# One eight-chunk loop for layer norm, transposes and all four projections, with affine, gates and norms in slots 2 to 5

## The chip, the core and the metric

The kernel runs on one core of a Trainium2 chip. A core has five engines with queues of their own: PE (TensorE, matrix products into PSUM), DVE (VectorE), ACT (ScalarE), POOL (GpSimd) and SP (SyncE, which here only issues DMAs). Each engine runs its instructions strictly in program order; between engines the order is made by semaphores. The metric is the device time of one execution in microseconds (us).

## The reference, cut to what matters

The input is 16 sequences of 256 tokens with 128 features, 4096 tokens in all. The output is the input plus an attention block plus a product-key expert block, both on the layer norm of the input.

```python
xn  = (x - mean) / sqrt(var + 1e-5)
# attention: 16 heads of 8 features
q   = xn @ Wq + bq
lat = xn @ Wl + bl;  k = lat @ Wk + bk;  v = lat @ Wv + bv
attn = softmax(q k^T / sqrt(8));  a = (attn v) @ Wo + bo
# experts: 8 heads, queries of 32 features
f   = xn @ fWq + fbq                       # 256 columns
f   = (f - mean(f)) / sqrt(var(f) + 1e-5) * gamma + beta   # over all tokens and heads
f0, f1 = l2norm of either half of f        # 16 features each
s0, s1 = f0 @ l2norm(key0)^T, f1 @ l2norm(key1)^T; top 4 of 32 in each
w   = softmax over the 16 sums;  idx = pairs of the top 4
out = sum_k w_k * gelu(down[idx_k] . xn) * up[idx_k]
return x + a + out
```

The mean and variance of `f` run over all tokens: no query can be scaled before the last chunk is projected.

## The kernel before: how it is tiled and what sets its order

The 4096 tokens are cut into eight chunks of 512 (`NC = 8`, `CH = 512`, four tiles of 128 tokens each). After a prologue loop over the chunks comes a software pipeline of "slots": slot n handles pair n of heads of the 128 pairs (`NPAIR * B`), eight to a sequence. Every engine's program holds both, written out by hand; nothing is reordered.

**Prologue loop.** For each chunk c DVE makes the mean and variance (lines 746 to 753), ACT the root (337), DVE the reciprocal and the shift `nm` (731, 733); ACT and DVE normalise two tiles each into `xn_sb` (326 and 739); PE transposes (462) into `psX`, ACT copies the result to `xnT` (334). One chunk later PE multiplies with fWq into `psF` (469), two halves r = 0, 1, which ACT copies to `fqT` (331) and of which DVE takes statistics with `bn_stats` (761). The matrices Wl and Wk, Wv are folded into `wkv` at c = 2 to 4 (473 to 478, copied by ACT at 317 to 319). Only chunks 0 and 1 are projected to q and k in or right behind this loop.

**Projections.** `project_qk(c)` and `project_v(c)` are three products with `wq_sb` and `wkv` (438, 441, 451) in PSUM `psQ`, `psK`, `psV`. DVE moves q and k to `q32` (`q_ev` 703, `k_ev` 710). Each fp32 value is then cut into three bf16 parts: ACT writes the first (303, in `first_parts`), POOL the residue `r32` (940, in `residues`), ACT the second (310, `second_parts`), POOL the third of q (942), DVE the third of k (`lo_k`, 714). `r32` has one buffer for q and one for k, so POOL's residue of a chunk waits until the third parts of the chunk before are made. SP writes the parts of a chunk to DRAM (`spill`, 245, six DMAs) and loads them back as rows of the heads (`load`, 262, twelve DMAs for a sequence). The parts have two buffers: `first_parts(c)` waits for `spill(c - 2)`. SP's queue, which the change leaves as it is, starts so:

```python
            spill(0)
            load(0)
            load(1)
            for c in range(1, NC):
                spill(c)
```

**Slots.** In each, PE makes the scores S of a pair (`si`, 526), DVE takes the row maxima `negm` (837), later (from slot 11) PE makes the transposed scores (586), ACT the exponential (413), PE the product with v (607). Chunks 2 to 7 are projected in slots 1 to 6, with their parts on ACT, POOL and DVE. Slot 0 solves for the scale of `f` (`bn_solve`, 802 to 813). In slots 0 to 7 DVE scales chunk `slot` of `fqT` in place (828, the affine), ACT squares it (367), PE sums the squares (`norms`, 539), and PE and ACT make the gates gelu(down . xn) (564, 362); `inverse_squares` (777, 780) turns sums of squares to inverses, a pair of chunks at a time. Until slot 10 the scores have one buffer `SI[0]`, because `SI[1]` holds v and the gates. POOL's residues stand in slots 0 to 6, and at slot 8 POOL adds the output bias to all of x in one instruction (954). From slot 8 on the experts' selection runs on DVE (881, 901), POOL (976 to 1019, 1039) and PE (634, 651), and `mpart` (1028, 1030) hands the maxima of a sequence over to PE (622).

Of the kernel before, what the change touches and what calls it, by code (L numbers as in the profile page):

```python
# [46 lines left out]
def program(nc, x, Wq, bq, Wl, bl, Wk, bk, Wv, bv, Wo, bo,  # L47
# [35 lines left out]
    with ctx:  # L83
# [45 lines left out]
        sq = Eb[:, 1, :].rearrange("p (r n) -> p r n", r=2)  # L129
# [160 lines left out]
        def _(act):  # L290
# [7 lines left out]
            def first_parts(c):  # L298
                if c >= 2:
                    act.wait_ge(s[f"spill{c % 2}"], 16 * NSPILL * (c // 2))  # L300
                for t, nm in enumerate(("q", "k")):
                    act.wait_ge(s[nm + "_ev"], c + 1)
                    A(parts[:, c % 2, t, 0, :], q32[:, t, :], ACT.Copy).then_inc(s["hi_" + nm], 1)  # L303
                    if t == 0 and c >= 1:
                        v_rows(c)

            def second_parts(c):
                for t, nm in enumerate(("q", "k")):
                    act.wait_ge(s["r_" + nm], c + 1)
                    A(parts[:, c % 2, t, 1, :], r32[:, t, :], ACT.Copy).then_inc(s["mid_" + nm], 1)  # L310

            for c in range(-1, NC + 2):
                if c == 4:

                    act.wait_ge(s["wkv"], 1)
                    act.wait_ge(s["w"], NW)
                    A(wkv[:, :, :], psW[:, 0:2 * D].rearrange("p (a d) -> p a d", a=2), ACT.Copy)
                    A(vecs[:, 8:9], psW[:, 2 * D:2 * D + 1], ACT.Identity, bias=vecs[:, 1:2])
                    A(vecs[:, 9:10], psW[:, 2 * D + 1:2 * D + 2], ACT.Identity, bias=vecs[:, 7:8]).then_inc(s["wkv_ev"], 1)
                if 0 <= c < NC:  # L320
# [7 lines left out]
                if c >= 2:  # L328
                    for r in range(2):
                        act.wait_ge(s["f"], 2 * (c - 2) + r + 1)  # L330
                        A(fqT[:, r, (c - 2) * CH:(c - 1) * CH], psF[c % 2][r], ACT.Copy).then_inc(s["f_ev"], 1)
# [746 lines left out]
```

## Time and profile before

| | us |
|---|---|
| median of three timed runs | 402.14 (401.37 to 403.36) |
| the profiled execution | 396.66 |
| its span, first to last instruction | 395.0 |

| engine | busy us | share of the span |
|---|---|---|
| PE | 330.2 | 84% |
| DVE | 347.4 | 88% |
| POOL | 248.0 | 63% |
| ACT | 244.3 | 62% |

The page has one line for each engine, with the span in 40 equal slices of 9.9 us; a digit is the busy share in tenths, and PEclk is TensorE's granted clock in tenths of full speed:

```profile
DVE  7769569999996999999999999999999999999571
ACT  2666438766746566666666666665756665656671
POOL 6003034776795676777586686767577677768780
PEclk9996989999858999999999999999999999999999
```

The first nine or ten slices are the prologue and slots 0 to 7, on which the change works; after some fourteen the pattern repeats.

### The profile page before, as it was taken

How to read it: one execution, taken by the hardware profiler on the slowest of the kernel's cores; microseconds unless marked ns; L12 is line 12 of the kernel's file. 1: busy time of each engine (PE TensorE's matmuls, PEld its weight loads, DVE VectorE, ACT ScalarE, POOL GpSimd, SP SyncE). 2: the span in 40 equal slices, each digit the busy share in tenths (PEclk: the TensorE clock that was granted, in tenths of full speed). 3: DMA queues.
4: the chain of work that ended last, by engine and by line, in shares of the span. 5: the costliest groups of instructions: out<-in, count | busy, mean ns of one | idle time of the engine just before them, and what ended most of it. 6: DMA issues, size and time to landing. Idle time of an engine off the chain costs nothing.

```text
span 395.0 us, 9652 instructions
## 1 busy us (share of the span) xinstructions
PE 330.2 (84%) x3080; PEld 175.2 (44%) x3080; DVE 347.4 (88%) x1446; ACT 244.3 (62%) x371; POOL 248.0 (63%) x527
## 2 busy tenths in 40 slices
PE   1877778885679898988989898898989898898874
PEld 0443444441325454544545454455445454454443
DVE  7769569999996999999999999999999999999571
ACT  2666438766746566666666666665756665656671
POOL 6003034776795676777586686767577677768780
PEclk9996989999858999999999999999999999999999
DMA  6401693445664150414235160515323060000000
GB/s 189 111 0 27 124 114 109 116 135 152 110 80 71 14 81 5 95 32 67 64 35 81 18 95 14 85 44 57 68 28 97 3 95 17 2 17 2 28 17 13
DMA packets 45886, 24.81 MB, mean 63 GB/s; under 512 B 5452, under 2 KB 45708, under 8 KB 45836
## 3 DMA queue, kind: packets, MB, share of 16 engines
q1 hardware_dynamic: 45836, 24.20, 33.1%
q8 instruction: 24, 0.39, 0.5%
q14 instruction: 26, 0.21, 0.2%
HBM read 15.54 MB, written 8.39 MB: 61 GB/s over the span
## 4 chain that ended last, share of the span: by engine, by line
PE 44%; DVE 20%; issue 5%; POOL 5%; ACT 2%; POOLq 0%; DVEq 0%
PE bank L607 11%; DVE negm L837 10%; PE bank L651 8%; PE bank L634 8%; PE SI L526 6%; DVE r_sb L901 6%; PE SJ L586 5%; PE bank L676 2%; ACT s_sb L381 2%; PE bank L677 2%; PE bank L678 2%; DVE rden L854 1%; DVE fqT L828 1%; POOL prod L1039 1%; PE bank L622 1%
## 5 line engine op out<-in xcount | busy, mean ns | idle before, releaser
L837 DVE TENSOR_REDUCE negm<-SI 128x4 f32<-128x1024 f32 x128 | 154.2, 1214 | 2.5 <-PE SI L526 2.5
L413 ACT ACTIVATE Eb<-SJ 128x1024 f32<-128x1024 f32 x128 | 130.3, 1018 | 32.0 <-PE SJ L586 31.8
L1039 POOL TENSOR_TENSOR prod<-r_sb,a 128x1024 f32<-128x1024 f32 x31 | 60.3, 1945 | 25.9 <-issue 25.9
L607 PE MATMUL bank<-Eb,vhat 128*18 128x256 f32 x1024 | 69.6, 390 | 0.0
L526 PE MATMUL SI<-KS,QS 48*128 48x256 bf16 x512 | 51.2, 279 | 19.5 <-DVE negm L837 17.3
L586 PE MATMUL SJ<-QS,KS 50*128 50x256 bf16 x512 | 51.7, 281 | 8.3 <-ACT Eb L413 8.1
L940 POOL TENSOR_TENSOR Eb<-Eb,parts 128x512 f32<-128x512 f32 x16 | 20.3, 1285 | 54.2 <-ACT parts L303 54.2
L881 DVE MAX8 top<-s_sb 128x8 f32<-128x32 f32 x512 | 50.4, 174 | 4.4 <-ACT s_sb L381 4.4
L901 DVE MATCH_REPLACE8 r_sb<-top,s_sb 128x36 f32<-128x36 f32 x256 | 43.1, 180 | 0.0
L526 PEld LDWEIGHTS SI<-KS,QS 48*128 48x128 bf16 x512 | 18.1, 96 | 54.5 <-issue 45.0
L651 PE MATMUL bank<-cst,prod 128*128 128x128 f32 x256 | 34.5, 278 | 4.2 <-ACT s_sb L381 3.7
L634 PE MATMUL bank<-kblk,fqT 128*128 128x256 f32 x128 | 37.1, 413 | 0.3
L607 PEld LDWEIGHTS bank<-Eb,vhat 128*18 128x18 f32 x1024 | 24.0, 98 | 27.3 <-issue 15.2
L651 PEld LDWEIGHTS bank<-cst,prod 128*128 128x128 f32 x256 | 27.5, 141 | 12.2 <-POOL prod L1039 7.0
L381 ACT ACTIVATE s_sb<-bank 128x512 f32<-128x512 f32 x32 | 19.1, 597 | 22.1 <-PE bank L634 20.1
L586 PEld LDWEIGHTS SJ<-QS,KS 50*128 50x128 bf16 x512 | 14.7, 95 | 36.4 <-ACT Eb L413 22.3
L634 PEld LDWEIGHTS bank<-kblk,fqT 128*128 128x128 f32 x128 | 22.2, 193 | 9.4 <-issue 3.8
L962 POOL COPY top<-top 128x32 f32<-128x32 f32 x32 | 6.7, 209 | 29.3 <-DVE top L881 29.3
L403 ACT ACTIVATE ysb<-bank 128x256 f32<-128x256 f32 x16 | 6.1, 383 | 28.4 <-PE bank L678 28.4
L846 DVE TENSOR_TENSOR wgT<-bank,xnT 128x256 f32<-128x256 f32 x16 | 6.8, 424 | 15.3 <-PE bank L651 15.3
L901 DVE MATCH_VALUE_LOAD r_sb<-top,s_sb 128x8 f32 x256 | 20.1, 79 | 0.0
L979 POOL TENSOR_TENSOR z_sb<-s_sb,rn 128x512 f32<-128x512 f32 x16 | 16.9, 1058 | 0.0
(149 smaller groups left out, 586.0 us busy)
## 6 DMA issues: line engine op xcount, KB each, us to landing
qk_parts<-parts SPq DMA_DIRECT2D x48, 128.0 KB, 2.4
QS<-qk_parts SPq DMA_DIRECT2D x32, 96.0 KB
KS<-qk_parts SPq DMA_DIRECT2D x32, 96.0 KB
x_sb<-L_attn_x SPq DMA_DIRECT2D x8, 256.0 KB, 3.7
QS<-qk_parts SPq DMA_DIRECT2D x32, 64.0 KB
KS<-qk_parts SPq DMA_DIRECT2D x32, 64.0 KB
out<-ysb SPq DMA_DIRECT2D x16, 128.0 KB, 4.2
QS<-qk_parts SPq DMA_DIRECT2D x32, 32.0 KB
```

The costliest lines, as they stand in the source:

```text
L381: A(s_sb[:, FH * t:FH * (t + 1), :, 0:NK].rearrange("p h a k -> p (h a) k"), psM.rearrange("p (g k) -> p g k", k=NK), ACT.Copy).then_inc(s ...
L413: A(Eb[:, n % 4, :], SJ[:, :], ACT.Exp).then_inc(s["ex"], 1)
L526: last = mm(si_buffer(n)[:, (e * BT + t) * S:(e * BT + t + 1) * S], QS[r, b % RING, pr, t * P:(t + 1) * P], KS[r, b % RING, pr, :], start= ...
L586: last = mm(SJ[:, (e * BT + t) * S:(e * BT + t + 1) * S], KS[r, b % RING, pr, t * P:(t + 1) * P], QS[r, b % RING, pr, :], start=True, stop ...
L607: last = mm(psO[32 * c:32 * c + 2 * VC, (q % 2) * S:(q % 2 + 1) * S], vhat[:, v0:v0 + 2 * VC], Eb[:, (2 * g + c // 2) % 4, e0:e0 + S], sta ...
L634: last = mm(psM[:, 256 * r:256 * (r + 1)], fqT[:, r, tok:tok + P], kblk[:, :, :].rearrange("p g k -> p (g k)"), start=True, stop=True)
L651: last = mm(psM[:, t * P:(t + 1) * P], prod[:, t, h, :, :].rearrange("p i j -> p (i j)"), ident, start=(h == 0), stop=(h == FH - 1), is_tr ...
L837: V.tensor_reduce(negm[:, bb % 2, :, :, pr].rearrange("p t e -> p e t"), si_buffer(slot)[:, :].rearrange("p (e t j) -> p e t j", e=2, j=S) ...
L881: last = V.max(top8[:, h, a, :], s_sb[:, h, a, 0:NK])
L901: last = V.match_replace(r_sb[:, h, :], top4[:, h, :], s_sb[:, h, 1, :], NEG)
L940: TT(r32[:, t, :], q32[:, t, :], parts[:, c % 2, t, 0, :], ALU.subtract).then_inc(s["r_" + nm], 1)
L1039: TT(prod[:, t, :, :, :], r_sb[:, hs, 0:NK].unsqueeze(2).to_broadcast([P, FH, TOP, NK]), a0[:, hs, :].unsqueeze(3).to_broadcast([P, FH, TO ...
```

## The change

One loop over the eight chunks now holds the layer norm, the transposes and all four projections: q, k and v of chunk c - 1 are made in iteration c, fWq of chunk c in iteration c itself. The splits into parts, `lo_k` and POOL's residues are in that loop as well (before, those of chunks 1 to 7 stood behind it or in the slots). `wkv` is folded at c = 0 and 1. The affine, the gates, the squares and the sums of squares of all chunks are done in slots 2 to 5, two chunks a slot. Scores have two buffers from the start and `si(n + 1)` is issued in slot n. `psF` has three buffers, `sq` has two. `bn_solve` is cut in two, in slots 0 and 1. POOL's addition of the bias to x stands at slot 0, right behind the residues of chunk 7. SP's queue isn't changed.

The diff, cut to its core:

```diff
             # ACT
+            deviations(0)
+            for c in range(NC + 1):
+                if c < NC:
                     act.wait_ge(s["nm"], c + 1)
...
                 if c + 1 < NC:
+                    deviations(c + 1)
+                if c < NC:
+                    act.wait_ge(s["xT"], c + 1)
+                    A(xnT[:, c * CH:(c + 1) * CH], psX[c % 2], ACT.Copy).then_inc(s["xnT"], 1)
+                if c == 1:
+                    act.wait_ge(s["wkv"], 1)
...
+                if c >= 1:
+                    first_part(c - 1, 0)
+                    first_part(c - 1, 1)
+                    v_rows(c - 1)
+                if c < NC:
+                    features(c, 0)
+                if c >= 1:
+                    second_part(c - 1, 0)
+                if c < NC:
+                    features(c, 1)
+                if c >= 1:
+                    second_part(c - 1, 1)
...
+            def first_part(c, t):
+                nm = "qk"[t]
+                act.wait_ge(s[nm + "_ev"], c + 1)
+                if c >= 2 and t == 0:
                     act.wait_ge(s[f"spill{c % 2}"], 16 * NSPILL * (c // 2))
...
+                if FILTER <= slot < FILTER + NC // 2:
+                    pair = (2 * (slot - FILTER), 2 * (slot - FILTER) + 1)
+                    for c in pair:
+                        act.wait_ge(s["g"], c + 1)
+                        A(gT[:, c * CH:(c + 1) * CH], psG[c % 2], ACT.Gelu).then_inc(s["g_ev"], 1)
...
+                    for c in pair:
+                        act.wait_ge(s["ff"], c + 1)
+                        if c >= 2:
+                            act.wait_ge(s["n2"], c - 1)
+                        A(sq[c % 2], fqT[:, :, c * CH:(c + 1) * CH], ACT.Square).then_inc(s["sq"], 1)
             # PE, in the loop, behind the transposes of chunk c
+                if c >= 1:
+                    project_qk(c - 1)
+                    project_v(c - 1)
+                if c < NC:
+                    pe.wait_ge(s["xnT"], c + 1)
+                    for r in range(2):
+                        i = 2 * c + r
+                        if i >= 3:
+                            pe.wait_ge(s["f_ev"], i - 2)
+                        mm(psF[i % 3], fwq_sb[:, r * P:(r + 1) * P], xnT[:, c * CH:(c + 1) * CH],
+                           start=True, stop=True).then_inc(s["f"], 1)
             # PE, in the slots
+            si(0)
             for slot in range(NSLOT):
...
+                if FILTER <= slot < FILTER + NC // 2:
+                    for c in (2 * (slot - FILTER), 2 * (slot - FILTER) + 1):
...
+                        mm(psG[c % 2], downT[:, :], xnT[:, c * CH:(c + 1) * CH], start=True, stop=True).then_inc(s["g"], 1)
...
+                if slot < NPAIR * B - 1:
                     si(slot + 1)
+                if FILTER <= slot < FILTER + NC // 2:
+                    norms(2 * (slot - FILTER))
+                    norms(2 * (slot - FILTER) + 1)
             # DVE, in the loop
                 if c + 1 < NC:
+                    moments(c + 1)
+                if c >= 1:
+                    q_ev(c - 1)
+                    k_ev(c - 1)
                     for r in range(2):
+                        dve.wait_ge(s["f_ev"], 2 * (c - 1) + r + 1)
+                        V.bn_stats(fst[:, r, c - 1, :], fqT[:, r, (c - 1) * CH:c * CH]).then_inc(s["f_st"], 1)
...
+                if c >= 2:
+                    lo_k(c - 2)
...
+            lo_k(NC - 1)
             # DVE, in the slots
+                if FILTER <= slot < FILTER + NC // 2:
+                    for c in (2 * (slot - FILTER), 2 * (slot - FILTER) + 1):
+                        fc = fqT[:, :, c * CH:(c + 1) * CH]
...
+                if slot == 0:
+                    bn_shift()
+                if slot == 1:
+                    bn_scale()
+                if FILTER < slot <= FILTER + NC // 2:
+                    inverse_squares(slot - FILTER - 1)
             # POOL
-            residues(0)
+            for c in range(NC):
+                residues(c)
             for slot in range(NSLOT):
                 k = slot % 8
                 b = slot // 8 - 1
-                if slot < NC - 1:
-                    residues(slot + 1)
-                if slot == NC:
+                if slot == 0:
                     pool.wait_ge(s["w2"], NW2)
                     pool.wait_ge(s["xn"], NC)
```

## Rows read from the trace of the kernel before

**Rows 1.** Windows: stretch, length, busy us (xcount) of PE, PEld, DVE, ACT, POOL; clock, DMA.

```profile
0.00:55.00 55.00, 35.13 (x113) 18.50 (x114) 39.04 (x148) 28.91 (x65) 12.85 (x14) 0.93 0.44 91
55.00:97.00 42.00, 33.08 (x242) 16.24 (x244) 41.82 (x53) 29.89 (x46) 24.18 (x20) 0.97 0.50 126
...
137.00:345.00 208.00, 189.27 (x2032) 102.45 (x2028) 199.14 (x918) 134.60 (x191) 149.78 (x363) 1.00 0.31 51
```

**Rows 2.** Timeline (start us, us, engine, instruction): DVE's maxima of slots 8, 24, 32.

```profile
96.79 1.23 DVE L837 TENSOR_REDUCE negm<-SI 128x4 f32<-128x1024 f32 x1
...
136.70 1.21 DVE L837 TENSOR_REDUCE negm<-SI 128x4 f32<-128x1024 f32 x1
...
154.31 1.22 DVE L837 TENSOR_REDUCE negm<-SI 128x4 f32<-128x1024 f32 x1
```

**Rows 3.** Timeline, prologue: first norm, first fWq products, copy of wkv, q product.

```profile
7.19 0.88 ACT L326 ACTIVATE Eb<-x_sb,ve,rs 128x128 f32<-128x128 f32 x2 [0.44 <-DVE ve L733]
...
11.59 3.62 PE L469 MATMUL SI<-xnT,fwq_sb 128*128 128x512 f32 x4
...
22.54 0.38 ACT L317 ACTIVATE wkv<-SJ 128x256 f32<-128x256 f32 x1 [2.81 <-PE SJ L478]
...
27.31 1.02 PE L438 MATMUL SJ<-xnT,wq_sb 128*128 128x512 f32 x2
```

**Rows 4.** Groups of DVE instructions, 0 to 100 us: count | busy us, mean ns | idle.

```profile
L828 DVE TENSOR_SCALAR fqT<-fqT,bnv 128x512 f32<-128x512 f32 x16 | 16.8, 1091 | 0.0
...
L761 DVE BATCH_NORM_STATS2 fst<-fqT 128x6 f32<-128x512 f32 x16 | 10.4, 682 | 2.7 <-ACT fqT L331 2.7
L746 DVE BATCH_NORM_STATS2 st<-x_sb 128x6 f32<-128x128 f32 x32 | 6.9, 276 | 0.0
L703 DVE TENSOR_SCALAR Eb<-SJ,vecs 128x512 f32<-128x512 f32 x8 | 5.9, 739 | 0.5 <-PE SJ L438 0.5
...
L714 DVE TENSOR_TENSOR parts<-Eb,parts 128x512 bf16<-128x512 f32 x8 | 5.7, 717 | 0.0
L739 DVE TENSOR_SCALAR Eb<-x_sb,mv,rs 128x128 f32<-128x128 f32 x16 | 4.8, 340 | 0.0
```

**Rows 5.** Single lines and timeline: DVE beside POOL instructions (durations min/median/max in ns).

```profile
L733 DVE SCALAR_TENSOR_TENSOR ve<-mv,rs x8: 161/161/1016, 7.0 to 35.9; 128x4 f32<-128x4 f32 x8
...
35.71 1.15 POOL L942 TENSOR_TENSOR parts<-Eb,parts 128x512 bf16<-128x512 f32 x1 [3.58 <-ACT parts L310]
35.87 1.02 DVE L733 SCALAR_TENSOR_TENSOR ve<-mv,rs 128x4 f32<-128x4 f32 x1
...
L828 DVE TENSOR_SCALAR fqT<-fqT,bnv x16: 533/1345/1385, 55.5 to 93.7; 128x512 f32<-128x512 f32 x16
...
381.06 2.89 POOL L1039 TENSOR_TENSOR prod<-r_sb,a 128x1024 f32<-128x1024 f32 x1
...
382.22 1.76 DVE L921 TENSOR_TENSOR prod<-prod,p0r 128x8 f32<-128x8 f32 x1
```

**Rows 6.** Timeline: POOL's addition of the bias to x.

```profile
97.16 8.83 POOL L954 TENSOR_TENSOR x_sb<-x_sb,bo_sb 128x4096 f32<-128x4096 f32 x1
```

**Rows 7.** Timeline of SP's queue: spill of chunk 0, first and last of the loads.

```profile
36.89 4.12 SPq L245 DMA_DIRECT2D qk_parts<-parts  x6
42.76 1.03 SPq L262 DMA_DIRECT2D QS<-qk_parts  x3
...
52.04 1.24 SPq L262 DMA_DIRECT2D KS<-qk_parts  x3
```

**Rows 8.** Groups of ACT instructions, 0 to 100 us: count | busy us, mean ns | idle.

```profile
L303 ACT ACTIVATE parts<-Eb 128x512 bf16<-128x512 f32 x16 | 9.9, 620 | 2.1 <-DVE Eb L710 1.6 <-DVE Eb L703 0.5
L367 ACT ACTIVATE Eb<-fqT 128x1024 f32<-128x1024 f32 x8 | 8.4, 1052 | 5.1 <-DVE fqT L828 2.8 <-PE bank L539 2.2
```

**Rows 9.** Timeline, slots: sums of squares, and PE behind POOL's maxima of sequence 1.

```profile
59.01 0.64 PE L539 MATMUL bank<-Eb,cst 128*32 128x128 f32 x16
...
118.16 0.39 PE L622 MATMUL bank<-cst,mpart 128*32 128x128 bf16 x2 [1.19 <-POOL mpart L1030]
```

More of the change, by code:

```diff
@@ L296, in v_rows, with second_part, features, deviations @@
                 A(v_tiles(c, c + 1)[:, :, 0:DH], psV.rearrange("p (n v) -> p n v", v=DH), ACT.Copy).then_inc(s["v_ev"], 1)
-            def first_parts(c):
-                if c >= 2:
+            def first_part(c, t):
+                nm = "qk"[t]
+                act.wait_ge(s[nm + "_ev"], c + 1)
+                if c >= 2 and t == 0:
                     act.wait_ge(s[f"spill{c % 2}"], 16 * NSPILL * (c // 2))
[L301 to L320, printed above, removed]
+                A(parts[:, c % 2, t, 0, :], q32[:, t, :], ACT.Copy).then_inc(s["hi_" + nm], 1)
+            def second_part(c, t):
+                nm = "qk"[t]
+                act.wait_ge(s["r_" + nm], c + 1)
+                A(parts[:, c % 2, t, 1, :], r32[:, t, :], ACT.Copy).then_inc(s["mid_" + nm], 1)
+            def features(c, r):
+                i = 2 * c + r
+                act.wait_ge(s["f"], i + 1)
+                A(fqT[:, r, c * CH:(c + 1) * CH], psF[i % 3], ACT.Copy).then_inc(s["f_ev"], 1)
+            def deviations(c):
+                act.wait_ge(s["var"], c + 1)
+                A(sd[:, TC * c:TC * (c + 1)], ve[:, TC * c:TC * (c + 1)], ACT.Sqrt).then_inc(s["std"], 1)
+            deviations(0)
+            for c in range(NC + 1):
+                if c < NC:
                     act.wait_ge(s["nm"], c + 1)
@@ L419, in _ @@
                     A(mT[:, :], psM[0:2 * H, 0:S], ACT.Copy).then_inc(s["mt_ev"], 1)
[L420 removed]
+                if slot == FILTER + NC // 2:
                     act.wait_ge(s["n2r"], NC // 2)
@@ L580, in _ @@
                         pe.wait_ge(s["kone"], 32)
-                        pe.wait_ge(s["q_ev"], NC)
-                        pe.wait_ge(s["k_ev"], NC)
+                        pe.wait_ge(s["g_ev"], NC)
                     for t in range(BT):
@@ L726, in unit_keys, with moments @@
                 last.then_inc(s["krep"], 1)
-            for c in range(-1, NC + 3):
-                if 0 <= c < NC:
+            def moments(c):
+                dve.wait_ge(s_x[c], 16)
+                tiles = range(TC * c, TC * (c + 1))
+                for n in tiles:
+                    last = V.bn_stats(st6[:, n, :], x_sb[:, n, :])
+                last.then_inc(s["stats"], 1)
+                dve.wait_ge(s["stats"], c + 1)
+                for n in tiles:
+                    last = V.bn_aggr(mv[:, n, :], st6[:, n, :])
+                last.then_inc(s["aggr"], 1)
+                dve.wait_ge(s["aggr"], c + 1)
+                V.tensor_scalar(ve[:, TC * c:TC * (c + 1)], mv[:, TC * c:TC * (c + 1), 1],
+                                LN_EPS, None, ALU.add).then_inc(s["var"], 1)
+            moments(0)
+            for c in range(NC + 1):
+                if c < NC:
                     dve.wait_ge(s["std"], c + 1)
@@ L796, in _, with bn_shift @@
                             grp.unsqueeze(2).to_broadcast([P, 8, NK]), ALU.mult).then_inc(s["kblk"], 1)
-            k_ev(1)
-            def bn_solve():
+            lo_k(NC - 1)
+            def bn_shift():
                 dve.wait_ge(s["ba"], 2)
```

175 lines of the change are left out of this document (46 added, 129 removed).

## The prediction

> **What bounds the kernel now.** I read the page's engine lines first, then the busy times of four long windows, then the timeline of the prologue and the first slots engine by engine, and last the single DVE lines whose longest duration is far above their shortest. In the repeating part, DVE is busy 199.14 of 208 us [rows 1]: it is the bound, and a sequence of eight slots takes 154.31 - 136.70 = 17.6 us [rows 2]. The change doesn't touch that part. DVE works in program order and has nothing to make up with, so whatever shifts slot 8 on DVE shifts the end. I therefore forecast when the maxima of slot 8 start: at 96.79 before [rows 2]. Slots 8 to 24 then take 39.9 us, 4.7 more than two sequences of 17.6.
>
> Between 55 and 97 us DVE seems full as well, 41.82 of 42 us [rows 1], but a part of that is waiting. An affine instruction takes 0.53 us at best and 1.35 at the median [rows 5]; sixteen take 16.8 us [rows 4] where 8.5 would do. The long ones stand beside POOL's residues. The same holds for tiny ones: the shift `nm` takes 0.16 us, and 1.02 once, when it came 0.16 us after a POOL instruction of 1.15 us had begun; it ended with it [rows 5]. Near the end, DVE's sum on 128x8 elements needs 1.76 us while POOL's product, itself held up by DVE, runs until 383.95 [rows 5]. So a DVE instruction of these kinds (scaling SBUF to SBUF, or two inputs in SBUF) and one of POOL exclude each other. The maxima, `bn_stats` and everything that reads PSUM don't wait.
>
> **The change part by part.** All starts below are us from the start of the span; a(c) is when ACT starts to normalise chunk c.
>
> *The first chunks.* ACT starts at 7.19 as before [rows 3]. Its queue now holds both copies of `features(0)` ahead of chunk 1. The four records of the first fWq products took 3.62 us [rows 3], at about half the rate of later ones (1.02 us for two [rows 3]). Transposes end near 9.3, the copy near 9.9, the products at 13.5, the copy, `wlT` and then a(1) at 14.4 (9.7 before). From there: norm 0.9, transposes 0.8, folding of wkv 1.2, its copy at 17.3 (22.54 before [rows 3]) and two small ones until 18.1, then q, k and v on PE (about 2.9) until 21, and five copies of 0.55 to 0.62 us [rows 8]: a(2) = 24.2. Bounds 23 to 26, by PE's rate.
>
> *The loop's period.* DVE does per chunk 4 x 0.28 + 2 x 0.34 for the norm, 2 x 0.74 for `q_ev` and `k_ev`, 2 x 0.68 for statistics, 0.67 to 0.72 for `lo_k` [rows 4] and seven small ops of about 0.16 [rows 5]: 6.4 us, about 6.2 start to start. ACT has nine such ops of 0.5 to 0.6 plus the norm, 6.0 us [rows 8], less than DVE. POOL's two residues and the third part of q are 1.15 us each [rows 5]. They exclude DVE's `nm`, its two normalised tiles and `lo_k`. By program order `lo_k` of chunk c - 2 releases the residue of k of chunk c - 1. DVE's next step is the reciprocal and then `nm`, which finds that residue running (about 1.0 us left, as in [rows 5]); then the third part of q gets in and the normalised tiles wait 1.1 us. I take 1.8 of these 2.1 us: period 8.0. Bounds 6.2 (no wait falls badly) and 8.6. Before, these waits were in the affine, 8.3 us in all.
>
> *SP's queue.* It is unchanged, but its neighbours moved. `spill(0)` can end only when `lo_k(0)` is done, which is last in DVE's iteration 2: a(2) + 6.4 = 30.6. Three DMAs (half of 4.12 us [rows 7]) and landing (42.76 - 41.01 = 1.75 [rows 7]) make 34.4. Then come 24 loads, which took from 42.76 to 53.28 = 10.5 us to issue [rows 7], then `spill(1)`, 4.1 + 1.75: landed at 50.8. ACT's first part of chunk 3 writes into the buffer that `spill(1)` reads. It is due in iteration 4, at a(4) + 3.75 = 24.2 + 16.0 + 3.75 = 44. It waits 6.9 us, and behind it in ACT's queue stand v, `features(4)` and the norm of chunk 5, for which PE and DVE wait. Before, the first parts of chunk 3 stood in slot 2, far behind the loads, which were hidden. So a(5) = 50.8 + 4.25 = 55.1, a(6) = 62.6 (DVE has caught up, one period of 7.5), a(7) = 70.6. A faster loop only waits longer here: only three periods count. Bounds of the wait: 3 (loads issue faster) and 10 us.
>
> *The end of the loop.* `q_ev(7)` ends 9.2 us after a(7). Then a first part (0.65), POOL's residue of q (1.15), `lo_k(6)` (0.7), the residue of k and the third part of q (2 x 1.15 and handovers): POOL is free at a(7) + 14.8 = 85.4. What POOL does next is the addition to x, 8.83 us [rows 6]. Before, it ran from 97.16, where DVE only had maxima, a reciprocal, top-4 searches and reads of PSUM, none of which waited. Now DVE's next ops are `lo_k(7)` and `bn_shift`: two inputs in SBUF, or a scaling in SBUF. They wait until 94.2, about 8 us. PE can run only two scores ahead. The longest such wait that the trace shows is 1.76 us [rows 5]; that it holds for one of 8.83 is the step I have to extrapolate. Bounds 0 and 8.7; I take 8, because each wait shown went on to the end of the POOL instruction.
>
> The Trainium skill, SBUF — State Buffer, section "Who interferes with whom", states that VectorE and GpSimd share one pair of SBUF ports by an exclusive lock that is held for the whole instruction, and that a VectorE instruction with two SBUF inputs or in a two-port mode takes part in it. By that rule the wait is the full rest of the 8.83 us; by a wait capped at the 1.76 us of the trace the sum would be about 6 us lower.
>
> *Slots 0 to 7.* The rest of slot 0 takes 0.65 us, slot 1 starts at 94.9. Slots 2 to 5 hold on DVE 4 x 0.53 [rows 5] + 1.2 + 1.25 = 4.6 us at most; the affine no longer meets residues, which saves its 8.3 us. But PE and ACT pass the ball within each slot: two gate products (2 x 0.95), a gelu (0.6), two squares (2 x 1.0 [rows 8]), sums of squares (0.64 [rows 9]) = 5.15 us, and the next gate products stand behind these sums. So slots 1 to 7 take 1.6 + 4 x 5.15 + 1.25 (inverse) + 1.2 = 24.65, and 0.5 for PE starting at its lower clock (1.2 GHz) after the idle stretch. Bounds 20 (DVE alone) and 30 (PE at that clock throughout). Slot 8 starts at 120.0: 23.2 us later than before.
>
> *Slots 8 to 24.* One inverse (1.25) is no longer here, and POOL is free, so that its chain to `mpart`, behind which PE stood at 118.16 [rows 9], starts some 1.5 us earlier. Of the 4.7 us of excess I give back 2.7; bounds 0 and 4.7.
>
> **Sum.** +23.2 - 2.7 = +20.5 us. On the profiled execution: 396.66 + 20.5 = 417.2 (span 395.0, 1.7 lie around it). The timed runs' median is 402.14, 5.5 above the profiled one; I add the same difference there: **422.6**.
>
> **The rivals.**
> - *The long addition doesn't hold DVE.* Everything else as forecast; DVE resumes when the third part of q is done, 7.9 us earlier: 414.7. For it: no row shows a hold beyond 1.76 us. Against it: all shown waits end with the POOL instruction.
> - *The spill doesn't hold the loop.* If DMAs are issued in a way that `spill(1)` lands before 44 us, 6.9 us fall away: 415.7. Against it: SP is in order and its 10.5 us are in the trace.
> - *The loop keeps DVE fed, and it comes out faster.* DVE was busy 39.04 + 41.82 us up to 97 [rows 1]; without the 8.3 us of the affine's waits and some 2 of others, and with one more inverse, its own work up to slot 8 is about 72 us. Before, slot 8 started at 96.8, so some 25 us were waiting. If the loop's waits overlap (period 6.2, no stall by SP or POOL) some 18 us remain: slot 8 at 90, -6.8 - 2.7 = -9.5 us, 392.6. The point from which it decides: DVE must wait less than 27 us in all before slot 8; my forecast has 48. For it: before, DVE idled 16 of the first 55 us [rows 1] because the loop had too little work for it, and now the loop has more. Against it: the in-order queues above.
> - *PE stays at the lower clock through slots 2 to 5.* Each such slot takes 7.2 instead of 5.15 us: +8, 430.6. For it: PE idles for about 8 us right before.
>
> **How the numbers follow.** Forecast 0.62, the addition not holding 0.17, the spill not holding 0.10, PE's clock 0.05, faster 0.06. Both of the first two rivals at once, with a short period (-5), give 403 or so; that is the low side of the cases. The forecast's own bounds: period -5/+2, slots -4/+4, spill -4/+3, last term -2/+2.7. Range for 8 in 10: 407 to 431. A measurement of this kernel can tell about 0.5% from no change. Slower 0.91, the same 0.03 (the mildest corner of the bounds), faster 0.06.
>
> **What would show it.** In the timeline after: ACT's first part of chunk 3 idle for some 7 us with a DMA as releaser near 44 to 51 us; DVE's `lo_k(7)` or the first scaling of `bn_shift` with a duration of 7 to 9 us, ending with POOL's 8.83 us; affines of 0.53 us in slots 2 to 5; `nm` with durations around 1 us; maxima of slot 8 near 120. Wrong would be: a wait of under 2 us beside the long addition, a period near 6, or slot 8 before 105.

## The result and the profile after

The kernel after takes 428.35 us (median of four runs, 426.86 to 432.6) where the kernel before takes 401.75 on the same chip (396.86 to 403.36): ratio 1.072 [1.059, 1.086], +26.6 us. Forecast were 422.6 us and +20.5. The profiled execution took 428.03 us (span 426.4) against 396.66 (395.0) before, so between the two traces lie 31.4 us. Executions of one kernel spread over 4 to 9 us, the slower ones at a lower granted clock (before: 396.6 us at 0.965, 403.7 at 0.945), so a few us between two traces or medians can come from that alone; the ratios leave out runs more than 1.5% above the quickest of their kernel.

The engine lines of the page after (40 slices of 10.7 us, busy share in tenths):

```profile
DVE  7077817679868899999999999999999999999571
ACT  2366156541562666665666656766667656666671
POOL 5043134376000766877677676776767767777790
PEclk9998868885696699999999999999999999999999
```

DVE's unbroken run of nines starts at slice 15, 149 us (before: slice 14 of 9.9 us, 128 us). Ahead of it stand gaps: DVE shows a 1 in slice 6 (53 to 64 us), PEclk falls to 6 in slice 6 to 5 and 6 in slices 10 and 11 (96 to 117 us) and to 6 in slices 13 and 14, and POOL has nothing to do in slices 11 to 13. The windows after, with the columns of [rows 1]: the loop from a(2) on, the stretch of the long addition, slots 1 to 8, and the part that repeats.

```profile
26.40:93.30 66.90, 42.74 (x148) 23.79 (x148) 43.16 (x111) 35.45 (x72) 24.30 (x22) 0.85 0.48 104
93.30:102.60 9.30, 0.22 (x4) 0.00 (x0) 9.27 (x4) 0.00 (x0) 9.28 (x2) 0.52 0.38 103
102.60:132.00 29.40, 21.04 (x184) 9.54 (x184) 21.48 (x40) 15.75 (x20) 0.46 (x2) 0.79 0.00 1
...
172.00:380.00 208.00, 189.06 (x2030) 102.95 (x2030) 199.09 (x934) 133.19 (x188) 150.47 (x371) 1.00 0.31 51
```

DVE is busy 199.09 of 208 us in the repeating part, 199.14 before [rows 1]: nothing was lost or won there. In the loop DVE is busy 43.16 of 66.9 us, PE 42.74 and ACT 35.45: none of them is full. In the second row DVE shows 9.27 us busy with four instructions, and PE all but stands still (0.22 us) at a granted clock of 0.52.

The timeline after, single rows of ACT, SP, POOL, DVE and PE (start us, duration us, engine, line, instruction, [idle before, releaser]):

```profile
26.42 0.88 ACT L324 ACTIVATE Eb<-x_sb,ve,rs 128x128 f32<-128x128 f32 x2
...
26.80 1.92 SPq L242 DMA_DIRECT2D qk_parts<-parts  x3
...
32.33 1.80 SPq L242 DMA_DIRECT2D qk_parts<-parts  x3
35.88 1.03 SPq L259 DMA_DIRECT2D QS<-qk_parts  x3
...
44.27 1.50 SPq L259 DMA_DIRECT2D KS<-qk_parts  x3
...
54.87 1.15 ACT L300 ACTIVATE parts<-Eb 128x512 bf16<-128x512 f32 x2 [8.52 <-DMA qk_parts<-parts]
...
88.56 1.15 ACT L300 ACTIVATE parts<-Eb 128x512 bf16<-128x512 f32 x2 [1.69 <-DMA qk_parts<-parts]
...
93.33 9.25 POOL L947 TENSOR_TENSOR x_sb<-x_sb,bo_sb 128x4096 f32<-128x4096 f32 x1
...
95.15 7.45 DVE L799 TENSOR_SCALAR bnv<-bnv 128x2 f32<-128x2 f32 x1
102.64 0.16 DVE L800 TENSOR_TENSOR bnv<-bnv 128x2 f32<-128x2 f32 x1
...
104.86 3.78 PE L559 MATMUL SJ<-xnT,downT 128*128 128x512 f32 x4
...
112.23 2.93 PE L559 MATMUL SJ<-xnT,downT 128*128 128x512 f32 x4
...
118.31 1.98 PE L559 MATMUL SJ<-xnT,downT 128*128 128x512 f32 x4
...
131.97 1.23 DVE L831 TENSOR_REDUCE negm<-SI 128x4 f32<-128x1024 f32 x1 [0.89 <-PE SI L527]
...
167.93 1.22 DVE L831 TENSOR_REDUCE negm<-SI 128x4 f32<-128x1024 f32 x1
```

The last two rows answer to [rows 2]: the maxima of slots 8 and 24 start at 131.97 and 167.93, 35.2 and 31.2 us later than before. So the whole loss arises before slot 8, and 4.0 us of it come back by slot 24. The SP rows answer to [rows 7] (the two groups of three are the first spill, q and k), the POOL row to [rows 6], the row at 26.42 to the a(2) of the prediction.

Two DVE lines after that answer to [rows 5] and [rows 4] (durations min/median/max in ns, first and last start):

```profile
L824 DVE TENSOR_SCALAR fqT<-fqT,bnv x16: 448/542/548, 105.4 to 120.9; 128x512 f32<-128x512 f32 x16
L749 DVE TENSOR_SCALAR Eb<-x_sb,mv,rs x16: 335/765/1193, 7.1 to 77.4; 128x128 f32<-128x128 f32 x16
```

The affine (L824) takes 0.54 us where its median was 1.35, because no residue runs beside it any more. The normalised tiles (L749) now meet the residues instead: their total goes from 4.8 us [rows 4] to 11.6 for sixteen.

### The profile page after: what moved, and what is told of

It is laid out like the page before. It is cut to its first block, busy times and chain, and to the rows that moved or that the text cites. A ratio compares the mean times of both kernels' runs of the same rounds, so it can differ in the third digit from the quotient of the medians.

```text
span 426.4 us, 9652 instructions
## 1 busy us (share of the span) xinstructions
PE 337.2 (79%) x3080; PEld 180.6 (42%) x3080; DVE 353.2 (83%) x1446; ACT 245.0 (57%) x371; POOL 245.1 (57%) x527
## 4 chain that ended last, share of the span: by engine, by line
PE 53%; DVE 21%; ACT 9%; issue 8%; POOL 4%; SPq 3%; DMA 2%; POOLq 0%; ACTq 0%; DVEq 0%
PE bank L601 10%; DVE negm L831 9%; PE bank L629 8%; PE bank L646 7%; PE SI L527 6%; DVE r_sb L895 5%; PE SJ L580 5%; PE SJ L559 2%; ACT s_sb L386 2%; PE bank L671 2%; SPq L259 2%; PE SJ L444 2%; DMA qk_parts<-parts 2%; PE SJ L447 2%; DVE bnv L799 2%
## 5 line engine op out<-in xcount | busy, mean ns | idle before, releaser
L419 ACT ACTIVATE Eb<-SJ 128x1024 f32<-128x1024 f32 x128 | 130.5, 1019 | 32.8 <-PE SJ L580 32.7
L601 PE MATMUL bank<-Eb,vhat 128*18 128x256 f32 x1024 | 68.6, 386 | 0.0
L934 POOL TENSOR_TENSOR Eb<-Eb,parts 128x512 f32<-128x512 f32 x16 | 18.5, 1160 | 58.9 <-ACT parts L300 50.0
L527 PEld LDWEIGHTS SI<-KS,QS 48*128 48x128 bf16 x512 | 18.3, 96 | 51.5 <-issue 44.0
L386 ACT ACTIVATE s_sb<-bank 128x512 f32<-128x512 f32 x32 | 19.1, 598 | 24.6 <-PE bank L629 22.7
L698 DVE TENSOR_SCALAR Eb<-SJ,vecs 128x512 f32<-128x512 f32 x8 | 6.0, 750 | 28.0 <-PE SJ L444 28.0
L955 POOL COPY top<-top 128x32 f32<-128x32 f32 x32 | 6.8, 211 | 35.5 <-DVE top L875 35.5
L629 PEld LDWEIGHTS bank<-kblk,fqT 128*128 128x128 f32 x128 | 22.7, 197 | 9.7 <-issue 3.8
L300 ACT ACTIVATE parts<-Eb 128x512 bf16<-128x512 f32 x16 | 9.9, 629 | 24.7 <-DMA qk_parts<-parts 10.2
L408 ACT ACTIVATE ysb<-bank 128x256 f32<-128x256 f32 x16 | 6.2, 385 | 28.4 <-PE bank L673 28.4
L1021 POOL CAST mpart<-negm 128x32 bf16<-128x32 f32 x16 | 3.4, 212 | 31.3 <-DVE negm L831 31.3
```

The costliest lines, as they stand in the source:

```text
L386: A(s_sb[:, FH * t:FH * (t + 1), :, 0:NK].rearrange("p h a k -> p (h a) k"), psM.rearrange("p (g k) -> p g k", k=NK), ACT.Copy).then_inc(s ...
L419: A(Eb[:, n % 4, :], SJ[:, :], ACT.Exp).then_inc(s["ex"], 1)
L527: last = mm(SI[n % 2][:, (e * BT + t) * S:(e * BT + t + 1) * S], QS[r, b % RING, pr, t * P:(t + 1) * P], KS[r, b % RING, pr, :], start=Tru ...
L601: last = mm(psO[32 * c:32 * c + 2 * VC, (q % 2) * S:(q % 2 + 1) * S], vhat[:, v0:v0 + 2 * VC], Eb[:, (2 * g + c // 2) % 4, e0:e0 + S], sta ...
L629: last = mm(psM[:, 256 * r:256 * (r + 1)], fqT[:, r, tok:tok + P], kblk[:, :, :].rearrange("p g k -> p (g k)"), start=True, stop=True)
L934: TT(r32[:, t, :], q32[:, t, :], parts[:, c % 2, t, 0, :], ALU.subtract).then_inc(s["r_" + nm], 1)
```

## The experiments

The theory was the forecast's: four separate losses (SP's loads ahead of `spill(1)`, the long addition that holds DVE, a loop period above DVE's own work, the PE-ACT round trip in slots 2 to 5). Each was taken away by itself and then with others. The first rival was that they cover each other, so that removing one gains little. The second, for the period, was that it isn't DVE's waits for POOL but the order of PE's program. "Slot 8" is the start of DVE's maxima of that slot, 131.97 in the kernel after; differences are against the kernel after. Each group of kernels was timed beside its own runs of the kernel before (medians 399.4 to 402.1), to which the ratios refer; they are the surer comparison where two medians lie close.

**The addition late (e1_add_late).**

```diff
 # POOL, in the slots
-                if slot == 0:
+                if slot == NC:
                     pool.wait_ge(s["w2"], NW2)
```

> Edit of the changed kernel: POOL's addition of the bias to x goes back to slot 8. Theory (a running POOL instruction that reads SBUF keeps out DVE's scaling of bnv until it ends): that scaling falls from 7.45 us to 0.2, slot 1 starts 7 us earlier, the whole is 6.5 to 7.5 us faster (ratio to the changed kernel 0.983), since nothing in slot 8 on DVE needs that access. Rival (DVE waited there for another reason, or the time comes back because POOL is then late for the selection at slot 11): 0 to 3 us faster.

Measured: 418.55 us (417.03 to 423.36), ratio 1.047 [1.039, 1.055]: 9.8 us less. The profiled execution is the slowest of the four, 423.36. In it slot 8 starts at 123.65, 8.3 earlier, of which 1.5 were there already at a(7) (76.43 instead of 77.96), ahead of the edit. The timeline, DVE's first scaling and POOL's addition:

```profile
94.08 0.23 DVE L799 TENSOR_SCALAR bnv<-bnv 128x2 f32<-128x2 f32 x1
...
122.93 8.82 POOL L947 TENSOR_TENSOR x_sb<-x_sb,bo_sb 128x4096 f32<-128x4096 f32 x1
```

The same scaling of two elements a partition takes 0.23 us instead of 7.45. Where the 8.82 us of POOL stand now, the maxima beside them take 1.23 us as ever, and the searches and PSUM reads as long as elsewhere. The rival "the long addition doesn't hold DVE" is refuted.

**The addition in eight pieces at its place (e3_add_pieces).**

```diff
-                    TT(x_sb[:, :, :], x_sb[:, :, :], bo_sb..., ALU.add).then_inc(s["xb"], 1)
+                    for i in range(NC):
+                        xs = x_sb[:, TC * i:TC * (i + 1), :]
+                        last = TT(xs, xs, bo_sb..., ALU.add)
+                    last.then_inc(s["xb"], 1)
```

> Edit of the changed kernel: the same addition at the same place, cut into eight instructions on a chunk each (about 1.15 us each). Theory (access is held per instruction, and is handed over between instructions): the scaling of bnv lasts at most 1.3 us, its two followers up to 1.2 us each, and the first affines meet the last pieces; 3 to 6 us faster than the changed kernel. Rival (access goes with POOL being busy at all, or the Pool queue of instructions is served first): DVE waits for all pieces, 0 to 1 us faster.

Measured: 425.61 us (423.13 to 429.4), ratio 1.066 [1.057, 1.076]: 2.7 us less, about as much as single runs differ, but slot 8 starts at 126.81, 5.2 earlier. The timeline of POOL and DVE:

```profile
92.48 10.25 POOL L949 TENSOR_TENSOR x_sb<-x_sb,bo_sb 128x512 f32<-128x512 f32 x8
...
94.31 1.13 DVE L799 TENSOR_SCALAR bnv<-bnv 128x2 f32<-128x2 f32 x1
95.47 1.18 DVE L800 TENSOR_TENSOR bnv<-bnv 128x2 f32<-128x2 f32 x1
96.68 1.18 DVE L801 TENSOR_TENSOR bnv<-bnv,fmv 128x2 f32<-128x2 f32 x1
```

Each of the small operations now waits out one piece (a piece is 10.25/8 = 1.28 us) and gets in before the next. So the exclusion is by instruction and is handed over between two of them; the rival, that DVE waits for all pieces, is refuted. The gain in time is below the forecast 3 to 6 us. Cutting the work up bounds one wait, but every small operation pays again: place counts for more than size.

A rival has to be met here. In the trace of e1 slots 8 to 24 take 39.67 us where the kernel after takes 35.96, so the addition, now standing at slot 8, could have cost there what it gave back at slot 0. Four traces tell the two apart, the rows for slots 8 to 24 of e3 (addition early) and of e8 below (addition late):

```profile
126.80:166.50 39.70, 33.26 (x266) 15.64 (x266) 33.73 (x156) 20.48 (x27) 21.17 (x58) 0.67 0.45 62
...
115.20:150.70 35.50, 28.40 (x266) 14.36 (x266) 32.95 (x156) 20.42 (x27) 29.23 (x59) 0.83 0.50 69
```

The stretch is long in e1 (late) and e3 (early) and short in e8 (late) and in the kernel after (early). The place of the addition doesn't decide it. What goes with it is PE's granted clock: 0.67 in both long ones, 0.82 and 0.83 in both short ones, with PE busy for 33.3 against 28.4 to 28.9 us on the same work.

**The loads late (e2_loads_late).**

```diff
 # SP
-            spill(0)
-            load(0)
-            load(1)
-            for c in range(1, NC):
+            for c in range(NC):
                 spill(c)
+                if c == NC - 3:
+                    load(0)
+                    load(1)
```

> Edit of the changed kernel: SP issues load(0) and load(1) behind spill(5) instead of behind spill(0). Theory (ACT's first part of chunk 3 waits for spill(1), which stands behind 10 us of loads in SP's queue): the wait of 8.5 us before it is gone, the loop ends 7 to 8.5 us earlier, the whole is 6 to 8 us faster, unless the first scores then wait for load(0), which is hidden behind POOL's long addition. Rival (spills themselves are too slow for the loop): a later first part waits instead, under 3 us faster.

Measured: 416.73 us (416.09 to 420.9), ratio 1.046 [1.036, 1.056]: 11.6 us less, more than the forecast 6 to 8; slot 8 at 120.84. ACT's wait at chunk 3 is gone, and a(7) comes at 69.39 instead of 77.96. The end of the loop on DVE:

```profile
88.41 1.23 DVE L831 TENSOR_REDUCE negm<-SI 128x4 f32<-128x1024 f32 x1 [4.29 <-PE SI L527]
...
89.73 3.08 DVE L799 TENSOR_SCALAR bnv<-bnv 128x2 f32<-128x2 f32 x1
```

The late `load(0)` makes a new wait of 4.29 us before the first maxima, and DVE, which by that wait arrives later at the scaling, is held for 3.08 us only. The two losses stand one behind the other and cover each other in part.

**Both (e4_add_and_loads): the edits of e1 and e2 together.**

> Both edits at once: addition to x at slot 8, and both loads behind spill(5). Theory (two separate stalls, one after the other on DVE's chain): the gains add up to 13 to 15 us, less 3 to 5 us by which the first scores now wait for load(0), which the long addition hid before: 9 to 12 us faster than the changed kernel, still 14 to 18 us slower than the kernel before. Rival (the stalls cover each other): no more than the larger of the two alone, 7 us.

Measured: 419.52 us (415.21 to 422.63), ratio 1.047 [1.036, 1.058]; slot 8 at 119.29. That is 1.6 us earlier than e2, and the median shows no gain over it (the forecast was 9 to 12 us below the kernel after, 8.8 were measured): with these loads, DVE waits 4.44 us for slot 0's scores in any case. The sum of the single gains, 8.3 + 11.1, is not reached.

**The loads spread and the addition late (e8_spread_add_late).** The first 24 loads go out as four groups of six, behind `spill(0)` to `spill(3)`; the addition as in e1.

```diff
 # SP
-            def load(b):
+            def load(b, es=(0, 1)):
...
-                for e in range(2):
+                for e in es:
...
-            spill(0)
-            load(0)
-            load(1)
-            for c in range(1, NC):
+            for c in range(NC):
                 spill(c)
+                if c < 4:
+                    load(c // 2, (c % 2,))
```

> Edit of the changed kernel: addition to x at slot 8, and the first two loads cut in four groups of six DMAs, one behind each of spill(0) to spill(3). Theory (two stalls, additive if the loads are neither in the way of spill(1) nor late for the first scores): no wait of over 2 us for a spill, no wait for load(0) (4.4 us with the loads behind spill(5)); maxima of slot 8 at 114 to 117, 14 to 17 us faster than the changed kernel. Rival (each group of six still delays a spill that is due): 8 to 12 us faster only, as with either edit alone.

Measured: 412.87 us (410.19 to 415.29), ratio 1.031 [1.022, 1.039]: 15.5 us less; slot 8 at 115.15, 16.8 earlier. Neither wait is left (only 1.68 us for the last spill). With nothing to cover them, the two are worth most of the sum of their single gains, 19.4.

**ACT normalises all four tiles (e5_act_norm).** This takes away the 11.6 us of L749 from DVE and its waits for POOL.

```diff
 # ACT
-                    for t in range(TC // 2):
+                    for t in range(TC):
 # DVE: the loop over the other two tiles, and PE's wait for it, are dropped
```

> Edit of the changed kernel: ACT normalises all four tiles of a chunk, so that DVE's two scalings per chunk, whose mean is 0.77 us instead of 0.34, are gone. Theory (the loop's period is made longer by DVE instructions that wait for POOL's residues): DVE saves 0.7 us of work and up to 1.7 of waiting per chunk, ACT gets 0.45 us more; periods of 9.4 to 9.9 us fall to about 8; but the wait for spill(1) grows by what the two chunks before it save, so only three periods count: 3 to 5 us faster. Rival (the period is set by the round trip PE, DVE, ACT, POOL and not by this access): periods stay above 9, 0 to 1 us faster or slower.

Measured: 435.54 us (431.51 to 435.86), ratio 1.085 [1.077, 1.093]: 7.2 us **more**. Two steps without a stall, a(5) to a(7), take 10.7 and 11.0 us, against 9.6 and 9.9. DVE's waits from 26 to 99 us (total, times, longest):

```profile
DVE Eb L697 <- PE SJ L444: 30.4, 7, 8.5
```

DVE got rid of its waits for POOL on these tiles and waited longer for PE's q product instead (18.4 us in the kernel after). The forecast of 3 to 5 us less was wrong in its sign. The reason that the forecast gave for the period falls: what binds is a chain that runs through ACT's norm, and the norm alone got 0.76 us longer (1.64 instead of 0.88) with each chunk. I read it in the trace of the kernel after, one iteration of chunks 5 and 6 on all engines:

```profile
58.44 0.88 ACT L324 ACTIVATE Eb<-x_sb,ve,rs 128x128 f32<-128x128 f32 x2
59.37 1.12 PE L466 MATMUL SI<-cst,Eb 128*128 128x128 f32 x4 [8.21 <-ACT Eb L324]
60.28 1.92 PE L444 MATMUL SJ<-xnT,wq_sb 128*128 128x512 f32 x2
62.23 0.75 DVE L698 TENSOR_SCALAR Eb<-SJ,vecs 128x512 f32<-128x512 f32 x1 [9.43 <-PE SJ L444]
63.02 0.63 ACT L300 ACTIVATE parts<-Eb 128x512 bf16<-128x512 f32 x1 [1.90 <-DVE Eb L698]
63.73 1.16 POOL L934 TENSOR_TENSOR Eb<-Eb,parts 128x512 f32<-128x512 f32 x1 [4.77 <-ACT parts L300]
65.39 0.68 DVE L709 TENSOR_TENSOR parts<-Eb,parts 128x512 bf16<-128x512 f32 x1
66.20 1.17 POOL L934 TENSOR_TENSOR Eb<-Eb,parts 128x512 f32<-128x512 f32 x1 [1.32 <-issue]
67.41 0.63 ACT L305 ACTIVATE parts<-Eb 128x512 bf16<-128x512 f32 x1 [0.44 <-POOL Eb L934]
68.04 0.86 ACT L324 ACTIVATE Eb<-x_sb,ve,rs 128x128 f32<-128x128 f32 x2
```

This is a ring: ACT's norm of chunk 5 at 58.44, PE's transposes, and only behind them, in PE's program, the q product of chunk 4; then DVE's `q_ev`, ACT's first part, POOL's residue, DVE's `lo_k`, POOL's residue of k, ACT's second part, and behind it in ACT's program the norm of chunk 6 at 68.04. The q product needs nothing of chunk 5 (its `xnT` was ready an iteration ago); it is late only by its place. Its 1.92 us, too, are nearly twice the 1.02 of [rows 3]: PE has idled 8.21 us before. That wait, and DVE's of 9.43, still hold the stall by the spill; in the next iteration, at 68.96 and 71.07, they are 2.85 and 1.10 us.

**The projections ahead of the transposes (e10_project_first): e8, and from c = 2 on PE makes q, k and v of chunk c - 1 first.**

```diff
 # PE, in the loop
             for c in range(NC + 1):
+                if c >= 2:
+                    project_qk(c - 1)
+                    project_v(c - 1)
                 if c < NC:
                     pe.wait_ge(s["xn"], c + 1)
...
-                if c >= 1:
+                if c == 1:
                     project_qk(c - 1)
                     project_v(c - 1)
```

> Edit of e8_spread_add_late: from chunk 2 on PE projects q, k and v of chunk c - 1 ahead of the transposes of chunk c, for which it waits on ACT and DVE. Theory (new, after ACT's extra tiles made the loop longer: the period is a round trip in program order, ACT's norm, PE's transposes, PE's q, DVE's q_ev, ACT's first part, POOL's residue, ACT's second part, ACT's next norm; DVE stands idle before q_ev, 9.1 us over seven chunks in e8): with q made before the transposes, ACT's waits for q_ev and k_ev (10 us over the chunks) go, periods fall from 8.6 to about 7.3 us, slot 8 comes 6 to 9 us sooner, the whole at 404 to 408. Rival (the access that DVE and POOL exclude each other from sets the period after all: DVE has 6.2 us of work and 2.3 of waiting): DVE's idle time turns into the same period, 0 to 2 us faster than e8.

Measured: 399.44, 406.48, 406.62 and 408.26 us, median 406.55; no ratio can be given, as three lie over 1.5% above the quickest. The trace is of the 406.48; in it slot 8 starts at 109.16, 6.0 earlier than in e8. Five periods from a(2) to a(7) take 35.4 us, 7.1 each, against 42.6 (8.5 each) in e8. DVE's waits between 25 and 75 us (total, times, longest):

```profile
DVE Eb L700 <- PE SJ L443: 1.4, 1, 1.4
```

Before `q_ev`, DVE waits once for 1.4 us; in e8 it was 9.1 us in seven waits, in the kernel after 18.4 (26 to 93 us), 9.4 of them by the spill's stall. The ring is cut, and the second rival, PE's order, is what set the period.

Up to slot 1 the gain is larger, 9.65 us (76.47 instead of 86.12); slots 1 to 8 then take 32.7 us instead of 29.0. PE's gate products of slot 4 here and in e11 below:

```profile
91.88 3.45 PE L561 MATMUL SJ<-xnT,downT 128*128 128x512 f32 x4
...
85.29 1.98 PE L561 MATMUL SJ<-xnT,downT 128*128 128x512 f32 x4
```

In e10 all four groups take 3.36 to 3.50 us, at a mean granted clock of 0.71 in the stretch, and the round trip is 6.7 us (91.88 to 98.61), not 5.13. This is the prediction's rival of PE's lower clock, come true in another kernel.

**The same order alone (e13_project_first_alone): the kernel after with this edit only.**

> The changed kernel with the order on PE of e10 alone: loads stay behind spill(0), addition at slot 0. Theory: the wait for spill(1) is set by SP's queue, so it grows by what the two chunks before it save: from 8.5 to 10.5 to 12 us; only three periods gain, 1.5 to 2 us each: 4 to 7 us faster than the changed kernel (421 to 425) where the same edit gave 6 us and more periods without the stall. Rival (SP's wait is not tied to the period): 8 to 12 us faster.

Measured: 420.91 us (418.02 to 424.04), ratio 1.052 [1.042, 1.062]: 7.4 us less; slot 8 at 126.40. ACT's row at chunk 3:

```profile
53.28 1.15 ACT L300 ACTIVATE parts<-Eb 128x512 bf16<-128x512 f32 x2 [11.20 <-DMA qk_parts<-parts]
```

a(3) and a(4) come 1.9 and 4.3 us earlier, but the wait for `spill(1)` grows from 8.52 to 11.20 us: of the 4.3 us won before the stall 1.6 are left at a(5). The rest of the gain comes from the periods behind it; the hold by the addition is 7.45 us as before. Slot 1 comes 9.2 us earlier, slot 8 only 5.6, for slots 1 to 8 take 32.7 us as in e10.

**The norms one slot later (e6_defer_norms).** PE makes the sums of squares of a pair of chunks a slot later, behind the next pair's gate products, so that ACT's squares have a slot's time.

```diff
 # PE, in the slots
                         mm(psG[c % 2], downT[:, :], xnT[:, c * CH:(c + 1) * CH], ...).then_inc(s["g"], 1)
+                if FILTER < slot <= FILTER + NC // 2:
+                    norms(2 * (slot - FILTER - 1))
+                    norms(2 * (slot - FILTER - 1) + 1)
...
-                if FILTER <= slot < FILTER + NC // 2:
-                    norms(2 * (slot - FILTER))
-                    norms(2 * (slot - FILTER) + 1)
```

> Edit of the changed kernel: PE makes the sums of squares of a pair of chunks one slot later, behind the gate products of the next pair. Theory (slots 2 to 5 are bound by a round trip: gate products, gelus, squares, sums of squares, next gate products, 5.1 us a slot where DVE has 4.3): slots 2 to 5 take 4.3 to 4.6 us each, the maxima of slot 8 come 2 to 3 us sooner. Rival (PE at its lower clock in these slots, or the inverses that now come a slot later, set the pace): within 1 us of the changed kernel.

Measured: 422.85 us (421.2 to 424.79), ratio 1.056 [1.049, 1.063]: 5.5 us less. Slots 1 to 8 take 23.3 us instead of 29.05. PE's timeline:

```profile
109.86 1.99 PE L559 MATMUL SJ<-xnT,downT 128*128 128x512 f32 x4
111.77 1.08 PE L540 MATMUL bank<-Eb,cst 128*32 128x128 f32 x32
...
113.11 1.98 PE L559 MATMUL SJ<-xnT,downT 128*128 128x512 f32 x4
```

The gate products follow each other after 3.25 us without a wait, where it was 5.13 in the kernel after: the round trip of the forecast is shown. DVE's affines now start 4.05 us apart (110.86 and 114.91): DVE's own work sets the slot. Not all that the trace shows is this edit's: of the 8.3 us by which slot 8 comes earlier, 2.5 are there before slot 1, and of the 5.75 in slots 1 to 8 some come from PE's clock, which was back by the second pair (gate products of slot 3 in 1.98 us instead of 2.93).

**All of it, and the sign of one edit.** e9_all_four is e8 with the edits of e5 and e6; e11_first_and_defer is e10 with that of e6; e12_first_defer_act is e11 with that of e5.

> All four edits: addition at slot 8, loads spread, ACT normalises, sums of squares a slot later. Theory: the gains add up, now with seven shorter periods instead of three: 22 to 28 us faster than the changed kernel, which is level with the kernel before (400 to 406). Rival (one loop with in-order round trips between four engines stays slower even without the four stalls): 408 to 415.

> The edit of e10 with the sums of squares a slot later (e6). Theory: the gain of e6 (5.5 us, from slots 1 to 8 taking 23.3 instead of 29.1 us) is in another stage and adds in full: 5 to 6 us below e10, 398 to 403, level with the kernel before. Rival (what follows slot 8 gives part of it back, because PE is idle more and comes to slot 8 at its lower clock): 2 to 4 us below e10.

> e11 with the edit of e5 on top: ACT normalises all four tiles. In the changed kernel this cost 7 us, because ACT's queue was part of the round trip and DVE stood idle. In e11 DVE is busy for 46.6 of the 50 us of the loop, 11.6 of them in ten scalings of 1.20 us that take 0.34 without POOL's residues. Theory (DVE with its waits for POOL is now what sets the period): DVE gets back up to 2.3 us a chunk and ACT, busy 36 of 50 us, takes 0.8: periods of 7.0 to 7.7 fall to 6.3 to 6.8, 3 to 5 us faster than e11: 393 to 396. Rival (ACT's queue is again the longer one, as in e5): periods of 7.8 or more, 2 to 6 us slower than e11.

Measured: e9 418.67 us, ratio 1.044 [1.036, 1.051], slot 8 at 121.72; its period is about 10 us, so ACT's tiles cost more than the later norms gained; both its forecasts (400 to 406, 408 to 415) were missed. e11 398.51 us (395.07 to 399.14), ratio 0.993 [0.989, 0.998], slot 8 at 99.16; the loop runs as in e10, and slots 1 to 8 take 22.7 us instead of 32.7, with PE's granted clock at 0.80 there instead of 0.71. That is more than the 5.75 us of e6. e12 **395.08 us** (393.94 to 396.61), ratio 0.990 [0.985, 0.994], slot 8 at 98.76. The window of e11 from 25 to 75 us (columns as above):

```profile
25.00:75.00 50.00, 37.17 (x148) 20.76 (x146) 46.60 (x113) 36.09 (x74) 25.59 (x22) 0.96 0.53 143
```

With the ring cut, DVE counts as busy for 46.6 of 50 us, a part of which is waiting for POOL: the ten normalised tiles in it take 11.6 us, where [rows 4] show 0.34 for one. Now the edit of e5 shortens the period: ACT's norms follow each other after 6.44 us instead of 7.1 (35.58, 42.02, 48.46 and so on). In e5 the same edit made it longer, 10.7 and 11.0 us instead of 9.6 and 9.9. So the forecast's reason for the period was a true one of the second rank: DVE's waits for POOL bind only when the ring doesn't. That e12 is quicker than e11 as a whole isn't shown: the shorter periods are lost in the first chunks (a(2) at 29.14 instead of 26.08, a(7) at 61.41 and 61.49), the profiled executions took 394.70 and 395.07 us, and the intervals of the two ratios overlap, though the medians lie 3.4 us apart.

e12 is 1% quicker than the kernel before. But its slot 8, at 98.76, is still 2.0 us later than the 96.79 of before [rows 2]. Between the two traces it is slots 8 to 24, 35.8 us instead of 39.9, that turn this into a gain of 2.0 us. So up to slot 8 the merged loop hasn't drawn level even with five edits, and no run shows why slots 8 to 24 are shorter.

## Why the prediction was right, and where it was short

- **The order of reading** (DVE bounds the repeating part, so the start of slot 8 decides): right. Slot 8 is 35.2 us late, slot 24 31.2, the span 31.4.
- **SP's queue:** right in place and size. The wait for `spill(1)` was 8.52 us (forecast 6.9), and the step from a(4) to a(5) 14.85 (14.9). e2 showed that the loads cause it. A second one, 1.69 us at the last chunk, was not foreseen.
- **The long addition:** right. The hold fell on the first scaling of `bn_shift`, 7.45 us (8), and ended at 102.60 with POOL's instruction (93.33 + 9.25). This was the step that had to be extrapolated from 1.76 us; e1 shows it by removal. By the rule of the Trainium skill, SBUF — State Buffer, section "Who interferes with whom", that was the full rest of POOL's instruction, and the trace agrees.
- **The affine's own time** fell to 0.54 us (0.53), and the 8.3 us of waits moved to the loop, as the prediction had it. They hit the two normalised tiles (2.30 us for a pair at 66.27 instead of 0.68) and not `nm`, which took 0.22 us in the mean.
- **The period:** this term was mis-sized, and its reason (DVE's own work and its waits for POOL) was the wrong one; what bound was the ring through PE's order. Forecast 8.0 from DVE's work and its waits; steps of 7.76, 9.41, 9.60 and 9.92 us were measured. From a(2) to a(7) it took 51.5 us instead of 46.4, +5.1. I had added up the work of the engines one by one, and never followed one value once round all five of them; e5 refuted the reason and e10 showed the right one.
- **The first chunks:** a(1) = 14.57 (14.4), but a(2) = 26.42 (24.2), +2.2. The copy of wkv came at 18.43 (17.3), and the q product took 2.08 us for its two halves where [rows 3] show 1.02: 1.1 and 1.1 us.
- **Slots 1 to 8:** 29.05 us instead of 25.15, +3.9. The round trip itself measured 5.13 (5.15; gate products at 118.31 and 123.44), and e6 shows it by removal. Missing was PE's clock: after 9.3 us with hardly any work the granted clock had fallen to 0.52, near the lower of its two levels (1.2 of 2.4 GHz), and the four gate products took 3.78 us in slot 2, 2.93 in slot 3 and 1.98 from slot 4 on. That alone is 2.75 us, where 0.5 was set aside. The rest I haven't divided up by runs.
- **The sum.** +2.2 (first chunks), +5.1 (period), +1.0 (end of the loop, with the second spill wait) and +3.9 (slots), less 0.4 because slot 1 followed the hold more closely, put slot 8 12.0 us later than forecast; 4.0 instead of 2.7 us came back by slot 24. Trace against trace the forecast is thus short by 10.9 us (31.4 against 20.5). In the medians it is short by 5.8 only, because the profiled execution before lay 5.1 us below its median and that after 0.3: the 5.5 us that I added to get from the one to the other weren't there a second time. A part of the closeness is luck.
- **Slots 8 to 24:** the reasons given for what comes back (one inverse fewer, POOL free for its maxima) are not shown. 4.0 us came back, but e3, with the addition and the inverses of the kernel after, took 39.72 us there, as much as before; PE's granted clock went with it, 0.67 against 0.82 (the kernel before took its 39.9 us at 0.79, so the clock alone may not explain it). That this term came near is luck, too.
- **The rivals.** "Not held by the addition" and "not held by the spill" are refuted. "PE at its lower clock" came true for the first pairs, not for all of slots 2 to 5. "The loop keeps DVE fed" failed by the in-order queues, as was said against it: slot 8 came at 131.97, not 90, and with five edits it comes at 98.76.

## What to carry to other kernels

When a loop is merged over several in-order engines, follow one value round all of them until the same engine starts the next iteration: that round trip, and not the fullest engine, was the period here, and three products moved ahead in PE's program brought slot 1 forward by 9.65 us and slot 8 by 6.0. A stall in an in-order queue swallows much of what is won ahead of it (8.52 became 11.20 us), so take away the stalls first and judge the sign of a balancing edit only then: the same four tiles on ACT made the period about 1.1 us longer in one surrounding and 0.7 shorter in another. Ask, too, in which stage a faster trace is faster: slots 8 to 24 took from 35.5 to 39.7 us wherever the addition stood, along with PE's granted clock. Put a long POOL instruction where DVE only reads PSUM or reduces.

## What the runs showed of the hardware

- A DVE instruction on 128x2 elements took 7.45 us while POOL's addition on 128x4096 ran, and 0.23 with nothing beside it. POOL's instruction was lengthened as well, from 8.82 to 9.25 us.
- With the addition in eight instructions, DVE got in between each two: 1.13, 1.18 and 1.18 us for three small operations.
- The two normalised tiles took 2.30 us a pair beside POOL's residues of 1.16, but the shift just ahead of them, which started at 66.19 where the residue started at 66.20, took 0.16: which of the operations pays is a matter of hundredths of a microsecond, and wasn't to be had from the trace of before.
- SP issued the six DMAs of the first spill in two groups of three, 1.92 and 1.80 us. The 3.6 us between them are a wait for `lo_k(0)`, which DVE ended at 32.31; before, the six took 4.12 us in all [rows 7]. The 24 loads behind them took 9.9 (35.88 to 45.77), 10.5 before.
- PE's four gate products took 3.78 us after 9.3 us with hardly any work and 1.98 at a granted clock of 1.00. On the same work in slots 8 to 24 PE was busy for 33.3 us at 0.67 and 28.9 at 0.82.
